# Score products of an attention kernel: two row tiles of 64 rows, one for each head, in place of one product of 128 rows with zero blocks

## The reference

```python
q = (x_q @ Wq + bq).reshape(b, sq, H, D_HEAD).transpose(0, 2, 1, 3)
k = (x_k @ Wk + bk).reshape(b, sk, H, D_HEAD).transpose(0, 2, 1, 3)
v = (x_v @ Wv + bv).reshape(b, sk, H, D_HEAD).transpose(0, 2, 1, 3)
s0 = jnp.einsum('bhqd,bhkd->bhqk', q, k) / math.sqrt(D_HEAD)
s0 = jnp.where(mask_mat, NEG, s0)
p = jax.nn.softmax(s0, axis=-1)
s1 = jnp.einsum('bhqk,bhkd->bhqd', p, v)
return s1.transpose(0, 2, 1, 3).reshape(b, sq, D_MID) @ Wo + bo
```

## Time and profile before

| | |
|---|---|
| median of 3 runs | 595.6 us (593.63 to 595.86) |
| the profiled execution | 595.16 us |
| its span in the profile | 593.4 us |
| PE busy | 548.5 us (92%) |
| DVE busy | 472.6 us (80%) |
| ACT busy | 393.6 us (66%) |
| POOL busy | 322.2 us (54%) |

### The profile page before, as it was taken

One profiled execution on the slowest core, in us unless ns is written; L12 is line 12 of the kernel. 1 busy time (PEld: TensorE's weight loads), 2 busy tenths in 40 slices (PEclk: granted clock), 3 DMA queues, 4 the chain that ended last, 5 costly groups with the idle time before them and its releaser, 6 DMA issues.

```text
span 593.4 us, 11881 instructions
## 1 busy us (share of the span) xinstructions
PE 548.5 (92%) x3880; PEld 506.5 (85%) x3880; DVE 472.6 (80%) x1338; ACT 393.6 (66%) x1054; POOL 322.2 (54%) x327
## 2 busy tenths in 40 slices
PE   6889999999999999999898997999779999969998
PEld 3778999999999899999786766899658788869998
DVE  5788878788888879896859996877798999965553
ACT  3876969696887859596834536477476667555552
POOL 7363754444554554533549879774088999810000
PEclk9899999999999999999999998999889999989999
DMA  8602000000110000000003332050077888614552
GB/s 212 201 2 72 2 2 2 1 2 1 34 58 2 2 2 2 1 2 2 2 20 158 150 134 108 20 199 1 2 276 256 285 281 267 231 35 147 177 176 71
DMA packets 35372, 53.36 MB, mean 90 GB/s; under 512 B 6157, under 2 KB 21457, under 8 KB 35313
## 3 DMA queue, kind: packets, MB, share of 16 engines
q1 hardware_dynamic: 35313, 52.61, 26.5%
HBM read 42.12 MB, written 10.49 MB: 89 GB/s over the span
## 4 chain that ended last, share of the span: by engine, by line
PE 59%; DVE 19%; POOL 8%; ACT 6%; issue 6%; DMA 1%; SPq 0%; DVEq 0%; POOLq 0%; ACTq 0%
PE ps L1458 8%; PE ps L1326 8%; PE ps L1387 8%; DVE w_gu_low L876 7%; PE ps L1277 6%; PE ps L1258 5%; PE ps L1310 5%; PE ps L1358 4%; PE ps L1289 3%; PE ps L1312 2%; POOL prob L599 2%; PE ps L1447 2%; DVE eo_high L1139 2%; ACT expo L730 2%; DVE hid L1126 1%
## 5 line engine op out<-in xcount | busy, mean ns | idle before, releaser
L599 POOL TENSOR_TENSOR prob<-expo,prec 128x512 f32<-128x512 f32 x64 | 66.9, 1045 | 97.3 <-DVE prec L992 96.1
L730 ACT ACTIVATE expo<-expo,nmin 128x154 f32<-128x154 f32 x256 | 106.2, 423 | 4.1 <-DVE nmin L981 3.6
L981 DVE CUSTOM_DVE_ANT_0 expo<-ps,maskb 128x154 f32<-128x154 f32 x256 | 69.2, 313 | 11.8 <-PE ps L1277 11.4
L660 POOL TENSOR_TENSOR wkq_low<-w_raw,wkq_high 128x1024 fp32r<-128x1024 f32 x16 | 51.3, 3209 | 27.5 <-ACT wkq_high L688 27.5
L1277 PE MATMUL ps<-kbd,qT_high 128*128 128x308 f32 x256 | 61.2, 323 | 0.3 <-ACT qT_high L669 0.3
L1001 DVE TENSOR_TENSOR pT_low<-ps,pT_high 128x512 fp32r<-128x512 f32 (+1 forms) x96 | 57.4, 598 | 4.2 <-ACT pT_high L744 3.8
L744 ACT CAST pT_high<-ps 128x512 fp32r<-128x512 f32 (+1 forms) x96 | 49.1, 515 | 15.5 <-PE ps L1289 11.8
L669 ACT ACTIVATE oT_high<-ps,bv_c 128x256 fp32r<-128x256 f32 x64 | 29.9, 468 | 36.8 <-PE ps L1312 36.8
L730 ACT ACTIVATION_READ_ACCUMULATOR expo<-expo,nmin 128x1 f32 x256 | 50.2, 196 | 0.0
L876 DVE TENSOR_TENSOR w_gu_low<-w_raw,w_gu_high 128x1024 fp32r<-128x1024 f32 x18 | 46.9, 2616 | 1.2 <-ACT w_gu_high L688 1.2
L1277 PEld LDWEIGHTS ps<-kbd,qT_high 128*128 128x128 f32 x256 | 40.1, 191 | 0.8 <-issue 0.5
(11 more groups left out here) (215 smaller groups left out, 1806.8 us busy)
## 6 DMA issues: line engine op xcount, KB each, us to landing
logits_dram<-lsb SPq DMA_DIRECT2D x16, 512.0 KB, 2.6
w_raw<-in_L_ffn_Wg_dram SPq DMA_DIRECT2D x16, 512.0 KB, 3.9
w_raw<-in_L_ffn_Wu_dram SPq DMA_DIRECT2D x16, 512.0 KB, 4.5
w_raw<-in_L_ffn_Wd_dram SPq DMA_DIRECT2D x16, 512.0 KB, 4.3
lraw<-logits_dram SPq DMA_DIRECT2D x16, 512.0 KB, 3.7
out_dram<-outb SPq DMA_DIRECT2D x16, 128.0 KB, 1.7
x<-in_x_dram SPq DMA_DIRECT2D x1, 1792.0 KB, 12.8
wk_raw<-in_L_xattn_Wk_dram SPq DMA_DIRECT2D x2, 512.0 KB, 5.0
```

Source lines behind the costliest of these rows:

```text
L599: pool.tensor_tensor(prob[:, n % 2, :, heads, :], expo[:, n % 2, pp, :, :, 0:P], prec[:, n % 2, pp].unsqueeze(3).to_broadcast([P, 2, 2, P] ...
L660: pool.tensor_tensor(low, w_raw[:, i % RAW].rearrange("p (k n) -> p k n", k=KD if w == 0 else FT), high, ALU.subtract).then_inc(gate_low i ...
L730: ins = act.activation(row, row, ACT.Exp, scale=-1.0, bias=nmin[:, n % 2, pp, j, h:h + 1], accum_out=psums[:, n % 2, pp, j, h:h + 1])
L981: ins = dve.tensor_tensor_reduce(out=expo[:, n % 2, pp, j, h, :], in0=ps[:, s % NS, h * SK:(h + 1) * SK], in1=maskb[:, (2 * (n // QUADS) + ...
```

## The change

The keys lose their zero blocks: `kbd` holds, for each batch, half and pair, 154 columns on all 128 partitions, head 0 above head 1. The score product becomes two matmuls of 64 rows by 154 columns, one for each head, on row tiles of the array: rows 0 to 63 and rows 64 to 127. They write to two banks, (2s + h) % 3. DVE raises `s_min` behind each head, ACT waits for each head by itself, and PE waits for `2 * s_i + 2 - NS` heads before S number s_i, that is for the first head of the S just before it. In the prologue the zeros go away, and K has one ACT and one DVE instruction of 128 partitions.

```diff
-    kbd = sb(att, "kbd", [P, B, 2, PAIRS, PK], F32R)
+    kbd = sb(att, "kbd", [P, B, 4, PAIRS, SK], F32R)
...
             if ev[0] == "zeros":
 
-                pairs = slice(2 * ev[1], 2 * ev[1] + 2)
-                link(pool.memset(kbd[0:DH, :, :, pairs, SK:PK].rearrange("p b s q k -> p (b s) q k").bitcast(F32), 0.0))
-                link(pool.memset(kbd[DH:P, :, :, pairs, 0:SK].rearrange("p b s q k -> p (b s) q k").bitcast(F32), 0.0))
-                pool.engine_nop().then_inc(zeros_ready, 1)
...
-                for at, cols, src in key_blocks(p, acc(no)):
-                    ins = act.activation(kbd[at, :, 0, p, cols], src, ACT.Identity, bias=bk_c[at, p:p + 1])
-                ins.then_inc(acc_high, 1)
+                act.activation(kbd[:, :, 0, p, :], keys_of(acc(no)), ACT.Identity, bias=bk_c[:, p:p + 1])\
+                    .then_inc(acc_high, 1)
...
-                act.wait_ge(s_min, s + 1)
                 for h in range(2):
+                    act.wait_ge(s_min, 2 * s + h + 1)
...
-                for at, cols, src in key_blocks(p, acc(no)):
-                    ins = dve.scalar_tensor_tensor(out=kbd[at, :, 1, p, cols], in0=src, scalar=bk_c[at, p:p + 1],
-                                                   in1=kbd[at, :, 0, p, cols], op0=ALU.add, op1=ALU.subtract)
-                ins.then_inc(acc_free, 1)
+                dve.scalar_tensor_tensor(out=kbd[:, :, 1, p, :], in0=keys_of(acc(no)), scalar=bk_c[:, p:p + 1],
+                                         in1=kbd[:, :, 0, p, :], op0=ALU.add, op1=ALU.subtract).then_inc(acc_free, 1)
...
                 for h in range(2):
-                    ins = dve.tensor_tensor_reduce(
-                        out=expo[:, n % 2, pp, j, h, :], in0=ps[:, s % NS, h * SK:(h + 1) * SK],
+                    dve.tensor_tensor_reduce(
+                        out=expo[:, n % 2, pp, j, h, :], in0=ps[:, (2 * s + h) % NS, 0:SK],
                         in1=maskb[:, (2 * (n // QUADS) + j) % TB], scale=-1.0, scalar=FAR, op0=ALU.add, op1=ALU.min,
-                        accum_out=nmin[:, n % 2, pp, j, h:h + 1])
-                ins.then_inc(s_min, 1)
+                        accum_out=nmin[:, n % 2, pp, j, h:h + 1]).then_inc(s_min, 1)
...
-                    pe.wait_ge(zeros_ready, n + 1)
-                if s_i >= NS:
-
-                    pe.wait_ge(s_min, s_i - NS + 1)
+                if 2 * s_i + 1 >= NS:
+
+                    pe.wait_ge(s_min, 2 * s_i + 2 - NS)
                 wait_high(pe, ("Q", n, pp))
-                dst = ps[:, s_i % NS, 0:PK]
                 for r, (s, m) in enumerate(LEFT_LAST):
                     if s == 1:
                         wait_used(pe, ("Q", n, pp))
-                    ins = pe.matmul(dst, qT[s][:, n % 2, pp, j * P:(j + 1) * P], kbd[:, b, m, p, :],
-                                    start=(r == 0), stop=(r == 2))
+                    for h in range(2):
+                        rows = slice(h * DH, (h + 1) * DH)
+                        ins = pe.matmul(ps[:, (2 * s_i + h) % NS, 0:SK], qT[s][rows, n % 2, pp, j * P:(j + 1) * P],
+                                        kbd[rows, b, m, p, :], start=(r == 0), stop=(r == 2))
                 ins.then_inc(s_full, 1)
```

More of the change, by code:

```diff
@@ L25 @@
 PROLOGUE = [
-    ("cT", 0), ("zeros", 0), ("warm", 4), ("zeros", 1), ("split", WK, 0), ("LN", 0), ("cT", 1), ("bk",),
+    ("cT", 0), ("warm", 4), ("zeros",), ("split", WK, 0), ("LN", 0), ("cT", 1), ("bk",),
     ("split", WQ, 0), ("K", 0), ("XN", 0), ("warm", 4), ("K", 1), ("xT", 0, 0), ("xT", 0, 1), ("mask",),
-    ("split", WK, 1), ("Q", 0, 0), ("K", 2), ("zeros", 3), ("split", WV, 0),
+    ("split", WK, 1), ("Q", 0, 0), ("K", 2), ("split", WV, 0),
 ]
@@ L39 @@
     ("S", 3, 1, 0): [("split", WO, 0)],
-    ("S", 0, 0, 1): [("zeros", 2), ("K", 5)],
+    ("S", 0, 0, 1): [("K", 5)],
     ("S", 4, 0, 0): [("split", WO, 1)],
@@ L60 @@
 LATER_POOL = {
-    "R1": 1, "SA": -0.5, "S10": -1, "T1": 5, "Q0": 1, "SB": -2, ("zeros", 0): -3, "PV1": 3, "Q1": 1, "XN": -3,
+    "R1": 1, "SA": -0.5, "S10": -1, "T1": 5, "Q0": 1, "SB": -2, "PV1": 3, "Q1": 1, "XN": -3,
     "xT1": -0.5, "T0": 2, "Y1": -2,
@@ L393, in program @@
     const_pool, const_dve, mask_ready = sem("const_pool"), sem("const_dve"), sem("mask_ready")
-    zeros_ready, bk_ready = sem("zeros_ready"), sem("bk_ready")
+    bk_ready = sem("bk_ready")
     acc_full, acc_high, acc_free = sem("acc_full"), sem("acc_high"), sem("acc_free")
@@ L447, in weight_half, with keys_of @@
         return [w[:, :, c * 512:(c + 1) * 512] for w in parts]
-    def key_blocks(p, src):
-        keys = src[:, 0:B * SK].rearrange("p (b s) -> p b s", b=B)
-        return [(slice(0, DH), slice(0, SK), keys[0:DH]), (slice(DH, P), slice(SK, PK), keys[DH:P])]
+    def keys_of(src):
+        return src[:, 0:B * SK].rearrange("p (b s) -> p b s", b=B)
     def keys_over(eng):
@@ L557, in step @@
             if ev[0] == "zeros":
-                pairs = slice(2 * ev[1], 2 * ev[1] + 2)
-                link(pool.memset(kbd[0:DH, :, :, pairs, SK:PK].rearrange("p b s q k -> p (b s) q k").bitcast(F32), 0.0))
-                link(pool.memset(kbd[DH:P, :, :, pairs, 0:SK].rearrange("p b s q k -> p (b s) q k").bitcast(F32), 0.0))
-                pool.engine_nop().then_inc(zeros_ready, 1)
[L563 to L569, removed]
+                link(pool.memset(quad_mask[:], 1.0))
+                link(pool.affine_select(out=quad_mask[:], in_=quad_mask[:], compare_op=ALU.is_ge, fill=0.0, base=0,
+                                        pattern=[[-TAIL, 4], [0, DH]], channel_multiplier=1))
+                pool.affine_select(out=quad_mask[:], in_=quad_mask[:], compare_op=ALU.is_ge, fill=0.0,
+                                   base=TAIL - 1, pattern=[[TAIL, 4], [0, DH]], channel_multiplier=-1)\
+                    .then_inc(const_pool, 1)
             elif ev[0] == "split" and ev[1:] not in LOW_DVE:
@@ L1350, in step @@
                 elif i == 0:
-                    pe.wait_ge(s_min, len(s_no))
+                    pe.wait_ge(s_min, 2 * len(s_no))
                     pe.wait_ge(t_free, len(t_no))
```

## The result

The changed kernel takes 671.66 us, median of 4 runs (666.74 to 673.58), against 595.49 us (593.63 to 595.86) for the kernel before on the same chip: a ratio of 1.127, 95% interval 1.121 to 1.134. The forecast was 670 us, in 634 to 695. The profiled execution took 666.74 us, with a span of 665.0, 71.6 more than before.

What follows compares the result with a forecast made beforehand. PE was taken to bound the kernel, busy 92% of the span and almost without pause in the attention. Span 593.4 + 45 + 6 + 25 + 2 - 3 = 668, then + 1.8 + 0.4 = 670 us, range 634 to 695.

Steps and rivals of the forecast that it cites:

- The bank wait: PE at S01 waits for DVE to read S00's first head, 45 us; S11 waits likewise for S10's, 6 us.
- S00 waits too: S00 on PE waits for S11's first head; no extra cost, since S01's wait is counted from T1's end.
- A change of tiling: PE going between full array and row tiles around S: 0.15 us each, 164 count, 25 us, at most 36.
- The products: Six 64-row matmuls of an S on PE: 0.45 us against 0.43, +2 us in all; bounds +23 and -9 us.
- Prologue: Before the attention, fewer ACT and DVE instructions on the keys shorten PE's wait: -3 us; dropped GpSimd memsets worth nothing.
- the group of 42 us: Sign in the profile after: four attention steps take near 42 us where they took 32.
- some 1.3 us in each step: Sign: PE idle at S01 some 1.3 us in each step, released by DVE's reading of the first head.
- Well under 1 us: Sign of a wrong forecast: S01's idle time well under 1 us, meaning DVE's order had let S00 ahead.
- PE's busy share in a group: Sign in the profile after: PE's busy share in the attention falls to near 80%.
- single file: Rival: six weight loads of an S on PE go one after another at 112 ns each, 691 us; chance 0.22.
- tiles cheap and side by side: Rival: tile changes on PE cost nothing and pairs run together at the pace of loads, 634 us; chance 0.18.
- the faster one: Rival: pairs side by side at 75 ns, loads hidden, no wait at S01, S takes 0.23 us, 566 us; chance 0.03.

Runs made afterwards that it cites:

- the bank wait alone: Kernel before, 128-row products and zero blocks kept, with signals by head and PE waiting for the first head of the S just before: 647.64 us, ratio 1.090.
- The six matmuls on the full array: Kernel before with the changed kernel's PE wait and signals, each S six matmuls of 128 rows by 154 columns into two banks, no row tiles: 666.38 us.
- tiles almost without pauses: Changed kernel with S01 behind PV0 from step 4 on, and DVE taking S10 and S11 sooner: 622.53 us, ratio 1.047.
- tiles doubled: Changed kernel with S01 behind PV0, S10 and S11 sooner on DVE, and each S computed twice into the same banks: 657.38 us.

## Why the prediction was right, and where by luck

The total was 670 for 671.7. Step by step:

- **The bank wait: right in mechanism and place, in size with some luck.** Forecast 45 + 6 = 51 us, measured 53.5 by the kernel that has nothing else. By place that kernel pays 1.62 us in a plain step where 1.5 were put, 1.30 behind a Y for 1.15, 1.83 where xT comes in for 1.5, and 1.55 at S11 in the step with the layer norm, where the rows gave 1.60 and half was taken. So a group pays 7.52 and not the 6.4 forecast. The total was close all the same because the first steps and the last group pay less (steps 0 and 1 together 27.8 us for 26.8). T1 stands ahead of S00 on DVE, and that sets it: in the timeline after, DVE has no backlog and the wait is there all the same, and where S00 was moved ahead of it on DVE, 0.30 us of it went.
- **S00 waits too**, 0.35 us in plain steps of the changed kernel. The forecast knew of this wait and held it swallowed by S01's, which is so: from T1 to PV0 it is 1.48 us more, 1.5 were forecast.
- **A change of tiling: 0.15 us forecast, 0.16 to 0.17 measured.** That number came from the 26-row transposes, a poor likeness, and was set roughly between 0 and 0.22; that it held so well is luck. The Trainium skill (TensorEngine Tiling (Array Packing), Key Properties) says that going from one tiling mode to another drains the engine; the runs agree, with 0.33 us for in and out together.
- **The products: the term that was wrong.** "I take the middle, for want of a row nearer to either", +0.02 us for an S. The bound was the truth: the tiles load and multiply side by side, three times 112 ns, and an S is 0.09 us shorter, -9 us where +2 was put. The 0.875 ns a column of the earlier trace rows gave the pace of the pairs well, 112 ns for 112 to 113 measured. The Trainium skill (TensorE: Matmul & The Clock Gate, Part 3) has matmuls of different row groups start some 4 ns apart; measured were 3.
- **The two together.** 25 + 2 = 27 us were forecast for tiles. At full clock they cost 40.97 - 39.65 = 1.32 us in a group over the bank wait alone, some 10 us in 8 groups. Of the difference to 27, 11 are the products'. The rest lies where PE waits. Beside the bank wait alone, the changed kernel comes to PV0 0.11 to 0.13 us sooner at each S01 (PV0 follows S01's first matmul after 0.49 us, 243.34 - 242.85, for 0.52, 172.79 - 172.27) and then loses 0.10 to 0.12 in PV0, so the tiles of S01 come out even; and from T2 to T1 in the step with the layer norm it takes 0.28 us less, where S11's wait is shorter by what S10 and its changes took longer before it. The forecast paid 0.17 and 0.32 us at these places.
- **The clock: no step at all.** The granted clock fell to half in ten stretches of the attention, 34.1 us together. At the price of the groups above, 42.50 with one such stretch, 44.02 with two and 44.87 with three, against 40.97 with none, one costs 1.3 to 1.5 us: about 14 us in the profiled execution. The other three runs, of 671.6 to 673.6 us, had a mean granted clock of 0.952 to 0.956 where this one had 0.967, so the clock also takes most of the 5 us between it and the median.
- **Prologue: -3 forecast, -2.4 measured.** The first S starts at 19.05 us instead of 21.43. PE's wait for DVE's keys fell from 2.5 us to 0.6. Other executions with the old prologue start their first S at 20.5 to 21.4 us, those with the new one at 18.5 to 19.4, so 2 is the better figure. That the memsets were worth nothing was not tested by itself.

The profiled execution then adds up to 53 + 10 + 14 - 2.4 = 75 us, where 71.6 were measured. Of the 3 us too much, about 1.4 are a stretch of half clock that the kernel with the bank wait alone has too, and 1.4 lie behind the attention, which the changed kernel passes in 286.0 us for 287.4, with three such stretches for five. The forecast had 51 + 27 - 3 = 75 over the span. So tiles were put 17 us too dear and the clock was forgotten with about 14, and these two hid each other. That the 670 came within 2 us is luck; that it was slower by more than 50 was not.

Of the smaller forecasts, the group of 42 us (40.97 at full clock) and the starts across changes further apart than within a stream (0.21 us into an S for 0.12 before) held. The idle time at S01 is released by DVE's first head as forecast, but "some 1.3 us in each step" is wrong: it is 0.72 in plain steps, 0.97 behind a Y and 1.37 where xT comes in. "Well under 1 us" was to be the sign of a wrong forecast, by way of a DVE that lets S00 ahead. In plain steps the number is under 1, but that is not what happened: another 0.35 stands at S00, and each wait costs some 0.27 us more than its idle time shows, since the record of the matmul before it runs on that long (S01 starts 0.99 us behind the last matmul of S00). PE's busy share in a group was put near 80% and is 35.44 / 40.97 = 87%, by the same records: only 5.53 of the 8.84 us stand as idle. Of the rivals, "single file" is refuted by the starts in pairs; "tiles cheap and side by side" was right in its second half and wrong in its first; the faster one would have needed the wait away, and even then (622.53) the changes alone keep it slower.

That the half clock comes from tiles and pauses together is only argued; what was seen stands in the last section.

## What to carry to other kernels

Before an instruction is split over more PSUM banks, count how many of its kind were in flight: here three banks for one each became three for two, and the lag of the reader, which had cost nothing, came to 1.3 to 1.8 us at each pair. Row tiles drop the zero blocks, but here one way in and out cost what about four S save; group the tiled products, or leave them alone. Changes that fell next to a wait were nearly free. And tiles with pauses brought a lower clock on top of both: read the granted clock of the profile after, before a sum that fits is believed.

## What was not expected of the hardware

**Two tiles behave like two queues.** With the heads one by one in the program, a second matmul starts 10 ns after the first of head 0, and all four products with `qT_high` start ahead of the one with `qT_low` of head 0, which stands third in the program. That the second to start is the first of head 1 is read from the pairs; the trace does not name the rows. Order within an S changed nothing (634.8 and 635.0 us). The loads of the three pairs of the S shown start 108 and 109 ns apart (at 205.899, 206.007 and 206.116). The first matmul's record starts with its load, those of the others some 70 ns behind theirs, so the second pair follows after 174 ns and the third after 113 more. The six matmuls on the full array show the same 174 where PE had waited before them, and 73 at S10, where it had not: in the starts, a change of tiles looks like a wait.

**A clock that falls.** Part of one group of the changed kernel by windows (as above), ahead of the fall, in it, behind it:

```profile
100.80:104.20 3.40, 2.03 (x21) 1.63 (x20) 2.86 (x17) 2.76 (x11) 0.70 (x2) 0.99 0.00 0
104.20:107.60 3.40, 3.40 (x18) 3.40 (x18) 1.30 (x5) 1.78 (x6) 1.36 (x2) 0.50 0.00 0
107.60:111.00 3.40, 3.40 (x32) 2.92 (x32) 1.80 (x9) 2.50 (x10) 0.27 (x1) 1.00 0.00 0
```

Ahead of the fall PE did S00 and S01 with their waits, 2.03 us of 3.40; then the granted clock is 0.50, 1.2 GHz, and PE, never idle, starts 18 matmuls where it starts 32 right behind at 2.4 GHz. Such stretches of 3.4 us in the attention, each counted in the one profiled execution of a kernel: changed 10, and 16 the second time; changed with S00 sooner on DVE, 5; the bank wait alone, with such pauses and matmuls of 128 rows, 1; six matmuls of 128 rows, with pauses, none; tiles with S01 behind PV0, 4; the same with the heads one by one, 2; tiles almost without pauses, 2, both in the first group, whose order was left as it was, pauses and all; tiles doubled, none; before, none. All executions, profiled or not, agree with this in their mean granted clock: 0.942 to 0.974 for the changed kernel, 0.979 and more for the bank wait alone, the six matmuls of 128 rows, the doubled tiles and the kernel before. So neither the pauses nor the 64-row matmuls alone brought them in number, the two together did. Why is open: no run changed the one by steps with the other held, and kernels that hardly differ gave 5, 10 and 16.
